# Vision tower on one core: five of eight feed-forward trees fetch their leaf rows instead of four, in two slot sets, with the order of calls chosen anew

## What is computed

```python
h = patches @ tok_W.T + tok_b                                  # (64, 196, 256)
h = h + attn(layernorm(h))     # gated attention: u * ((relu(qk / sqrt(128)) ** 2) @ v), then @ o_w.T
h = h + ffn(layernorm(h))

# ffn: 8 binary trees (PAR) of depth 7, 255 nodes each
logits = x @ W_in.T + b_in                     # (rows, 8 * 255)
decisions = logits > 0;  acts = silu(logits)
for d in range(7):                             # walk down: one child per level
    current = child of current, by its decision
masked = acts, only where the walk has passed  # 8 nodes of 255 per tree
out = masked @ W_out.T
```

## Time and profile before

| | us |
|---|---|
| median of 3 runs | 2025.92 (2025.3 to 2026.82) |
| the profiled execution | 2028.2 |
| its span, first to last instruction | 2026.4 |

### The profile page before, as it was taken

How to read it: one execution, slowest core, us unless ns; L and a number is a source line. 1 busy time by engine, 2 the same in 40 slices (tenths; PEclk the granted TensorE clock), 3 DMA queues, 4 the chain that set the end, 5 groups by cost and what they waited for, 6 DMA issues and landing times. The chain is left out here.

```text
span 2026.4 us, 41146 instructions
## 1 busy us (share of the span) xinstructions
PE 1973.2 (97%) x12488; PEld 1858.1 (92%) x12488; DVE 1702.8 (84%) x4210; ACT 1397.2 (69%) x3085; POOL 1001.6 (49%) x1001
## 2 busy tenths in 40 slices
PE   6799999999999999999999999999999999999997
PEld 5689999999999999999999999999999999999986
DVE  5598888898888898888898888898888898888875
ACT  5467776677776676776676776676776776776764
POOL 2675445545445545445545545545545545545544
PEclk8999999999999999999999999999999999999999
DMA  4423223223222223223233223232223233222222
GB/s 131 108 75 93 76 77 82 79 72 90 77 75 81 78 76 87 74 77 80 75 83 84 75 76 82 73 86 83 75 75 81 74 87 83 75 75 79 61 68 80
DMA packets 81999, 163.12 MB, mean 80 GB/s; under 512 B 17102, under 2 KB 48048, under 8 KB 81968
## 3 DMA queue, kind: packets, MB, share of 16 engines
q0 software_dynamic: 40960, 103.02, 19.3%
q1 hardware_dynamic: 41008, 59.71, 10.3%
HBM read 148.76 MB, written 13.90 MB: 80 GB/s over the span
## 5 line engine op out<-in xcount | busy, mean ns | idle before, releaser
L483 POOL DMA_INDIRECT leaf_rows<-leaf_table,leaf_at x512 | 582.2, 1137 | 156.0 <-issue 156.0
L861 DVE TENSOR_TENSOR hid_lo<-hid,hid_hi 128x392 fp32r<-128x392 f32 (+1 forms) x256 | 255.3, 997 | 77.3 <-ACT hid_hi L551 77.2
L1168 PE MATMUL out_acc<-hid_hi,outw_lo 128*128 128x392 f32 x768 | 300.3, 391 | 0.2 <-DVE hid_lo L861 0.2
L456 POOL TENSOR_TENSOR inv_root<-to_root,minus_half 98x8 f32<-98x8 f32 x64 | 95.7, 1495 | 412.7 <-DVE to_root L911 266.1
L1168 PE MATMUL hid_ps<-ffn_x,in_lo 128*128 128x392 f32 x768 | 272.1, 354 | 1.8 <-ACT hid L706 0.7
L1170 PE MATMUL out_acc<-hid_hi,outw_hi 128*128 128x392 f32 x768 | 263.4, 343 | 0.0
L1169 PE MATMUL hid_ps<-ffn_x,in_hi 128*128 128x392 f32 x768 | 262.8, 342 | 0.0
L1169 PE MATMUL out_acc<-hid_lo,outw_hi 128*128 128x392 f32 x768 | 262.2, 341 | 0.0
L1170 PE MATMUL hid_ps<-ffn_x,in_hi 128*128 128x392 f32 x768 | 261.4, 340 | 0.0
L496 POOL TENSOR_TENSOR row_sum<-leaf_rows,row_sum 98x1024 f32<-98x1024 f32 x96 | 221.3, 2305 | 40.3 <-ACT leaf_rows L743 34.6
L482 POOL TENSOR_TENSOR held<-minus_half 98x1 f32<-98x1 f32 x128 | 35.7, 279 | 373.6 <-ACT v_full L637 199.6
(11 more groups left out here) (142 smaller groups left out, 5854.6 us busy)
## 6 DMA issues: line engine op xcount, KB each, us to landing
x_raw<-x SPq DMA_DIRECT2D x192, 196.0 KB, 2.4
out<-out_stage SPq DMA_DIRECT2D x32, 392.0 KB
leaf_rows<-leaf_table,leaf_at POOLq DMA_INDIRECT x512
leaf_table<-leaf_rows SPq DMA_DIRECT2D x4, 256.5 KB, 4.2
out_stage<-in_w SPq DMA_DIRECT2D x4, 256.0 KB
tok_major<-tok_w SPq DMA_DIRECT2D x3, 256.0 KB, 4.3
late_raw<-out_w SPq DMA_DIRECT2D x6, 128.0 KB
u<-uv_w SPq DMA_DIRECT2D x1, 576.0 KB, 4.2
```

The source lines that it names most:

```text
L483: pool.indirect_dma_start(row_slot(s, g), None, table, bass.IndirectOffsetOnAxis(ap=leaf_at[:, s, g:g + 1], axis=0), element_offset=s * P ...
L861: dve.tensor_tensor(out, src, hi.bitcast(F32), ALU.subtract).then_inc(done, 1)
L1168: pe.matmul(out, w[1], x_parts[0], start=start, stop=False)
```

## The change

- `GATHERED` goes from 4 to 5: tree 4 is a gathered tree now and only 5, 6 and 7 are dense. `SUMS` follows (4 sums a unit).
- The slots: tree `s` uses the set `s % 2`, so one set serves trees 0, 2 and 4 and the other trees 1 and 3. The semaphore counts and the wait of the first trees of a unit follow: tree 0 waits for all sums of the unit before, tree 1 for all but the last.
- The pieces of late weights are one fewer and are split at other places.
- The lists of calls in all four `body` functions are in another order, and are cut at another place of the cycle. Some calls that stood at the end of `body` with `n` stand at its start with `i`, which is the same work.

The diff, cut to its core (the lists that are left out only reorder calls):

```diff
-GATHERED = 4
+GATHERED = 5
...
-LATE_SPLITS = (((0, 1), (2,), (3,), (4,), (5,)), ((6,), (7,), (8, 9), (10, 11), (12, 13)))
+LATE_SPLITS = (((0, 1), (2,), (3,), (4,), (5,)), ((6,), (7, 8), (9, 10), (11, 12), ()))
...
 
         def row_slot(s, g):
 
-            return leaf_rows[0:HALF, (GROUPS * s + g) % ROW_SLOTS]
+            return leaf_rows[0:HALF, GROUPS * (s % TREES_HELD) + g]
 
         def row_landed(i, s, g):
 
-            n = GROUPS * s + g
-            return rows_in[n % ROW_SLOTS], 16 * (GROUPS * GATHERED // ROW_SLOTS * i + n // ROW_SLOTS + 1)
+            part = s % TREES_HELD
+            uses = (GATHERED - part + TREES_HELD - 1) // TREES_HELD
+            return rows_in[GROUPS * part + g], 16 * (uses * i + s // TREES_HELD + 1)
 
...
                     elif not first(i):
-                        pool.wait_ge(rows_summed, SUMS * i + s + 1 - TREES_HELD)
+                        pool.wait_ge(rows_summed, SUMS * i - s)
...
-                at = GROUPS * s % ROW_SLOTS
+                at = GROUPS * (s % TREES_HELD)
...
             def body(p, i, n, nx):
+                sum_rows(p, 2)
+                fetch_rows(p, 4, 0)
+                fetch_rows(p, 4, 1)
+                fetch_rows(p, 4, 2)
+                fetch_rows(p, 4, 3)
+                norm_roots(i, 1)
+                sum_rows(p, 3)
+                norm_roots(n, 0)
                 late_splits(i, n, 0)
+                sum_rows(p, 4)
+                fetch_rows(i, 0, 0)
                 late_splits(i, n, 1)
-                sum_rows(p, 3)
-                fetch_rows(i, 0, 0)
-                late_splits(i, n, 2)
+                fetch_rows(i, 0, 2)
+                fetch_rows(i, 0, 3)
                 fetch_rows(i, 0, 1)
-                fetch_rows(i, 0, 3)
-                fetch_rows(i, 0, 2)
                 fetch_rows(i, 1, 0, n)
                 fetch_rows(i, 1, 1)
+                fetch_rows(i, 1, 2)
+                late_splits(i, n, 2)
+                fetch_rows(i, 1, 3)
+                fetch_rows(i, 2, 0)
                 late_splits(i, n, 3)
-                fetch_rows(i, 1, 3)
-                fetch_rows(i, 1, 2)
-                fetch_rows(i, 2, 0)
+                late_splits(i, n, 4)
+                fetch_rows(i, 2, 1)
                 fetch_rows(i, 2, 3)
-                fetch_rows(i, 2, 1)
                 fetch_rows(i, 2, 2)
-                late_splits(i, n, 4)
                 sum_rows(i, 1)
                 fetch_rows(i, 3, 0)
+                fetch_rows(i, 3, 3)
+                fetch_rows(i, 3, 1)
                 fetch_rows(i, 3, 2)
-                fetch_rows(i, 3, 1)
-                fetch_rows(i, 3, 3)
-                norm_roots(n, 1)
-                sum_rows(i, 2)
-                norm_roots(nx, 0)
 
...
             def body(p, i, n, nx):
-                silu_tree(p, 7, 1)
+                norm_apply(i, 1, 2)
+                norm_apply(i, 1, 3)
+                copy_h(n, 0)
                 ffn_x_high(i, 0)
                 ffn_x_high(i, 1)
-                silu_tree(p, 7, 0)
-                copy_h(n, 0)
                 copy_h(n, 1)
                 scale_rows(p, 3)
+                leaf_silu(p, 4)
+                scale_rows(p, 4)
                 hid_high(p, 7)
                 silu_tree(i, 0, 0)
+                silu_tree(i, 1, 0)
                 norm_apply(n, 0, 0)
-                silu_tree(i, 1, 0)
-                leaf_number(i, 0)
                 norm_apply(n, 0, 1)
                 make_xn(n, 0)
+                leaf_number(i, 0)
+                make_xn(n, 1)
+                norm_apply(n, 0, 2)
+                norm_apply(n, 0, 3)
                 hid_high(i, 0)
-                norm_apply(n, 0, 2)
-                make_xn(n, 1)
-                norm_apply(n, 0, 3)
                 make_xn(n, 2)
+                make_xn(n, 3)
                 silu_tree(i, 2, 0)
...
             def body(p, i, n, nx):
+                hid_low(p, 6)
+                ffn_x_low(i, 0)
+                ffn_x_low(i, 1)
+                mask(p, 7)
                 norm_stats(n, 0, 0)
                 norm_stats(n, 0, 1)
                 norm_moments(n, 0)
@@ -1081,72 +1093,69 @@
...
+                gate(n, 0)
                 decisions(i, 6)
-                square_relu(n, 1)
-                kern_low(n, 0)
-                v_low(n, 3)
-                kern_low(n, 1)
-                x_low(nx, 1)
-                hid_low(i, 4)
-                gate(n, 0)
-                mask(i, 5)
+                leaf_dots(i, 2)
                 gate(n, 1)
                 mix_low(n, 0)
                 gate(n, 2)
                 mix_low(n, 1)
                 mix_low(n, 2)
                 gate(n, 3)
+                mask(i, 5)
                 mix_low(n, 3)
-                leaf_dots(i, 2)
+                x_low(nx, 1)
+                decisions(i, 7)
                 mask(i, 6)
                 update_h(n, 0)
+                hid_low(i, 5)
                 update_h(n, 1)
-                decisions(i, 7)
                 x_low(nx, 2)
+                leaf_dots(i, 3)
...
+                embed(n, 5)
                 turn_ffn_x(i, 0)
                 turn_ffn_x(i, 1)
-                embed(n, 5)
+                tree_out(p, 5, 1)
                 tree_visits(p, 7)
-                tree_out(p, 5, 0)
                 turn_h(n, 0, 0)
                 turn_h(n, 0, 1)
-                tree_out(p, 5, 1)
                 tree_logits(i, 0, 0)
                 tree_logits(i, 1, 0)
+                tree_out(p, 6, 0)
                 tree_visits(i, 0)
-                tree_out(p, 6, 0)
+                tree_out(p, 6, 1)
                 tree_logits(i, 2, 0)
+                tree_visits(i, 1)
                 find_leaf(i, 0)
+                tree_logits(i, 3, 0)
                 if first(n):
                     turn_rows()
-                tree_visits(i, 1)
-                tree_out(p, 6, 1)
-                tree_logits(i, 3, 0)
+                tree_visits(i, 2)
```

181 lines of the change are left out of this document (89 added, 92 removed).

## The result

The changed kernel takes 2118.81 us (median of 4 runs, 2116.9 to 2125.64) where the kernel before takes 2026.19 on the same chip: a ratio of 1.0461, with a 95% interval of 1.0448 to 1.0474. The forecast was 2043 us with a range of 1985 to 2088. The direction was right, the size was wrong by a factor of more than five: +93 us, not +17. The profiled execution is the slowest of the four (2125.64 us), so what is summed from its rows comes out some 7 us above the median.

A forecast was written before the change was run, and what follows sets the result against it. TensorE, busy 97%, bounds the kernel: 59.05 + 0.15 + 1.4 + 0.55 + 0.3 = 61.45 us a unit, 0.5 more than now. Thirty units (15.3), head -2 and tail +4 give 2025.9 + 17.3 = 2043 us, range 1985 to 2088.

The forecast's parts named there:

- The work: TensorE per unit: 12 matmuls fewer (2.14 us), one find_leaf more (0.25 us), giving 59.05 us if nothing waits.
- The other engines: GpSimd, VectorE and ScalarE: despite added gathers, sum, dots and scalings, all stay below TensorE's 59 us a unit.
- First junction: turn_h(n,0) to tree_visits(i,0): sum_rows(p,3) lies over VectorE's moments, so TensorE waits 1.4 us more a unit.
- third zone: The mixing: tree 2's dots ahead of gate(n,1) make the gate late; charged 0.3 us, range 0 to 1.4.
- Second junction: tree_visits(i,2), directly behind tree_logits(i,3), waits for leaf_number(i,0) on ScalarE: 0.55 us of new wait a unit.
- rival (c): Mixing goes badly: sum 2 takes the port first or gathers are long; about 62.8 us a unit, 2084 us; chance 0.20 with GpSimd-bound case.
- The clock: TensorE: where one wait comes near 3 us, slower clock adds to it; eight transposes then took 1.57 us.
- The gather chain: Gather, landing, dots, scaling and sum end about 0.5 us ahead of norm_apply's turn; charged nothing, a miss up to 1 us.
- Head and tail: Outside the loop: head -2 us (0 to -4) from fewer late pieces, tail +4 us (2 to 8) from an added round.

The follow-up runs named there:

- k1: Kernel before, with sum_rows of tree 3 moved ahead of the next unit's norm_roots on GpSimd: 2074.37 us, ratio 1.0239.
- k4: Changed kernel: sum 2 waits for x_low(nx,1), scale_rows(i,3) behind silu_tree(i,7,0), leaf_number(i,0) directly behind silu_tree(i,1,0): 2067.32 us, ratio 1.0195.
- k11: Changed kernel: sum_rows(p,3) behind norm_roots(n,0), sum 2 waits for x_low(nx,1), leaf_number(i,0) directly behind silu_tree(i,1,0): 2096.72 us, ratio 1.0343.
- k12: k11 with x_low(nx,5) ahead of leaf_dots(i,4) on VectorE: 2091.04 us, ratio 1.0331.
- k15: Changed kernel: leaf_number(i,0) earlier, scale_rows(i,3) behind x_high(nx,5), sum 3 waits for hid_low(p,6), sum 2 for x_low(nx,1): 2042.35 us, ratio 1.0081.
- k9: Changed kernel in which sum 2 alone adds 8 of 256 columns, the rest left out: 2055.08 us, ratio 1.0140.
- k3: Changed kernel with tree 3's row scaling moved earlier on ScalarE, behind silu_tree(i,7,0): 2126.11 us, ratio 1.0483.
- k7: k4 with x_low(nx,5) ahead of leaf_dots(i,4) on VectorE and late_splits(i,n,2) behind fetch_rows(i,1,3) on GpSimd: 2155.62 us, ratio 1.0627.
- k2: Changed kernel where sum 2 on GpSimd also waits for x_low(nx,1): 2082.40 us, ratio 1.0278.
- k18: k15 with sum 2 waiting for mix_low(n,3), x_low(nx,1) behind mask(i,6), x_low(nx,5) ahead of tree 4's last dot: 2055.47 us, ratio 1.0129.
- k8: Changed kernel with late_splits(i,n,2) behind fetch_rows(i,1,3) on GpSimd: 2132.10 us, ratio 1.0502.
- k13: Changed kernel with late_splits 2, 3 and 4 all behind the gathers of tree 2 on GpSimd: 2129.83 us, ratio 1.0511.
- k5: Changed kernel where each of the four GpSimd sums adds 8 of 256 columns, the rest left out: 2012.19 us, ratio 0.9936.

## Why the prediction was right or wrong

**The work.** Counted at -1.89 us a unit, measured at about -1.8: right. The other engines stayed below their limits, as said. One figure there is wrong without consequence: by the count's own terms (30.1 + 8.0 of 59 us) GpSimd has 21 us free, not 15.

**`turn_h(n,0)`.** Counted at +0.15 us, measured at +0.5 (0.66 against 0.15); it waits for `ffn_x_low`, which comes later than my count had it.

**First junction.** Right in mechanism and size: a moment step over 1 us was forecast (1.38 measured), 1.4 us of added distance at `tree_visits(i,0)` (1.26 measured, 1.40 against 0.14), and k1 shows it alone. The rule of the Trainium skill ("SBUF — State Buffer", section "Who interferes with whom"), that the second of two such instructions waits for all of the first, agrees with these rows too. In the third zone it can't be read off who was second, since the held operation is recorded as the first.

**Second junction.** Counted at 0.55 us; the two distances behind `find_leaf` and ahead of `tree_visits(i,2)` are 0.53 together. The size is right by luck, the mechanism by half. In k4, k11, k12 and k15, where `leaf_number(i,0)` is earlier, the 0.28 us ahead of `tree_visits(i,2)` go, so these are the wait that was forecast. The 0.25 us behind `find_leaf` stay in all of them, so they are something else, which the count didn't have and no run explains.

**Third zone.** This is the step that failed. It was charged 0.3 us, for a late `gate` behind the dots of tree 2; no wait at `mix` came, so that term measured nothing. I left the meeting of `sum_rows(i,2)` with `x_low(nx,1)` to rival (c), because by my count the two start within 0.1 us, and took it to cost nothing if the sum begins just behind. The sum does begin behind, by 0.20 us (1089.41 against 1089.21), and `x_low` still ends only behind the whole sum. And on both sides of the near tie stands an operation with two SBUF operands: the sum catches either `x_low(nx,1)` (1.5 us at `embed` and `turn_h`) or `mix_low(n,3)` ahead of it (2.15 us at `project_o`), and which of the two goes with some 10 ns. The order had no good outcome, and k9 prices it at 2.3 us a unit with the clock, where the forecast had 0.3. The price of the first junction, charged for each of the four sums in turn, would have given it: 61.45 - 0.3 + 1.5 to 2.15 is 62.7 to 63.3 us, +51 to +71 us in the loop. That k9, which takes the third zone away, has the forecast's period (61.43 against 61.45) is partly luck: `turn_h(n,0)` is 0.35 us more than counted, and `tree_visits(i,0)` 0.14 and the `gate` 0.3 us less.

**The clock.** I named it in rival (c) for waits near 3 us. Here it came behind 1.87 us, in 7 of 30 units, for 1.55 us each: some 11 us in the changed kernel, and more in k3 and k7, where 19 and 29 of the 30 units took over 64.5 us.

**Rival (c)** had the cause right and was too small: 2084 us, since it counted one such case at 1.35 us a unit and left out both the clock and the worse of the two kinds. Its chance of 0.20 was too low.

**The gather chain**, charged nothing with "a miss costs up to 1 us": right in the changed kernel, where no wait shows it, presumably because the collisions elsewhere give it time. As soon as they are gone (k2, k4, k11 to k18) it is the next limit, at 0.4 to 1.2 us a unit (in k11 and k12 beside the wait at `add_rows`).

**Head and tail.** The tail was +5.7 us for +4 (2 to 8 allowed): right. The head was +7.6 where I said -2, a wrong sign: I counted fewer pieces to split and not that a fifth tree's gathers share GpSimd with those splits in a stretch where it is busy for 27.7 of 30 us. That GpSimd is short there is seen; that this alone makes the 7.6 us was not shown, since k8 and k13 gained nothing.

## What to carry to other kernels

Where an engine works beside GpSimd, take each long GpSimd operation on SBUF and ask for its whole possible window, not for its likely start, which two-operand operations of VectorE lie in it or just ahead of it; if one stands on either side of a near tie, charge the collision in full. A cost that is taken off an order of calls without slack turns up one link further: price a repair by the next wait in the chain, and test the upper bound first by shrinking the suspected operation in place, as k5 did. And a wait of over 1 us on TensorE, in this kernel, can bring a stretch at half clock behind it: it did so each time at 2.0 us in k7 (29 of 29) and in 7 of 16 waits of 1.83 to 1.87 us in the changed kernel's loop.
